# One step of a learning loop in a new order: gradients in one piece, weights 20 from an early sum

## What is computed

```
def _mlp(params, h):                      # params: (w1_0, w2_0), (w1_1, w2_1); hidden width 256
    for w1, w2 in params:
        h = h + gelu(h @ w1) @ w2
    return h
assoc_loss = lambda p, k, v: mean((_mlp(p, k) - v) ** 2)
def step(carry, x_t):                     # 32 steps, one after the other
    params, mom = carry
    k, v = l2norm(x_t @ Wk), x_t @ Wv
    lr, forget, eta = ...                 # one number for each image
    g = grad(assoc_loss)(params, k, v)
    new_mom    = eta * mom - lr * g
    new_params = params * (1 - forget) + new_mom
```

## Time and profile before

| what | before |
|---|---|
| median of 3 runs | 959.83 us (956.37 to 960.83) |
| the profiled execution | 957.53 us, its span 955.7 us |
| busy, share of the span | PE 85%, DVE 76%, ACT 65%, POOL 64% |
| the learning loop | about 72 to 564 us of the span |
| before it, `prepare`; behind it, read-out, attention, experts | 72 us; 392 us |

### The profile page before, as it was taken

The page is one execution under the profiler, slowest core; times in us unless marked ns, Lnnn a source line. Parts: engine busy times, 40 slices in busy tenths (PEclk is TensorE's granted clock), DMA queues, the critical chain, the costliest instruction groups (busy, mean ns, idle before and its releaser), DMA issues. The chain is left out here.

```text
span 955.7 us, 25199 instructions
## 1 busy us (share of the span) xinstructions
PE 809.4 (85%) x8049; PEld 506.4 (53%) x8049; DVE 726.0 (76%) x1861; ACT 618.9 (65%) x1384; POOL 608.6 (64%) x758
## 2 busy tenths in 40 slices
PE   2788999999999999999999989965678777999950
PEld 2455555555555555555555544431246544999940
DVE  3586888888888888888888871578798875777747
ACT  4577777778777787877777753228823523888830
POOL 1127888878788887878788739940004777666650
PEclk8899999999999999999999999987998978999985
DMA  7006999996000000000000005005000113233327
GB/s 239 1 2 140 159 208 158 81 6 2 0 0 0 0 0 0 0 0 0 0 0 0 0 5 157 18 11 185 1 4 29 52 51 90 82 93 93 92 68 239
DMA packets 105406, 54.10 MB, mean 57 GB/s; under 512 B 42624, under 2 KB 96664, under 8 KB 105360
## 3 DMA queue, kind: packets, MB, share of 16 engines
q1 hardware_dynamic: 98976, 43.34, 28.9%
q0 software_dynamic: 4544, 9.38, 3.0%
q10 hardware_dynamic: 1840, 0.79, 0.3%
HBM read 21.49 MB, written 29.44 MB: 53 GB/s over the span
## 5 line engine op out<-in xcount | busy, mean ns | idle before, releaser
L398 POOL TENSOR_TENSOR s_w<-s_xsh,s_w_mem 128x512 f32<-128x512 f32 x186 | 252.0, 1355 | 9.0 <-DVE s_w_mem L570 3.5
L570 DVE SCALAR_TENSOR_TENSOR s_w_mem<-s_w_mem,s_eta,lp_g 128x256 f32<-128x256 f32 x496 | 218.0, 476 | 23.9 <-PE lp_g L733 18.6
L495 ACT ACTIVATE s_xsh<-s_w,l_keep_lr 128x256 f32<-128x256 f32 x384 | 173.9, 507 | 17.5 <-POOL l_keep_lr L418 17.5
L1489 POOL DMA_INDIRECT f_yg<-f_yr,f_xmeta x78 | 78.3, 1004 | 38.4 <-DVE f_yr L1857 25.6
L1484 POOL DMA_INDIRECT f_xg<-f_xrow,f_place x64 | 64.0, 1000 | 49.3 <-DVE f_place L1750 30.4
L403 POOL TENSOR_TENSOR s_xsh<-s_w,l_keep 128x512 f32<-128x512 f32 x64 | 72.0, 1125 | 0.0
L1464 ACT ACTIVATE f_hh<-fp_v,f_bcol 128x256 f32<-128x256 f32 x156 | 61.4, 476 | 14.4 <-DVE f_hs_lo L1848 8.5
L489 ACT COPY l_wt<-lp_b 128x512 f32<-128x512 f32 x96 | 56.5, 588 | 15.0 <-PE lp_b L719 15.0
L719 PE MATMUL lp_b<-s_cst,s_w 128*128 128x128 f32 x384 | 61.7, 284 | 0.0
L1594 PE MATMUL fp_v<-f_xf,s_w_hi 128*128 128x256 bf16 x312 | 54.4, 276 | 3.3 <-DVE f_xmeta L1837 2.7
L707 PE MATMUL lp_h<-s_w,l_gf 128*32 128x128 f32 x1024 | 41.4, 278 | 18.3 <-ACT l_gf L482 18.3
(11 more groups left out here) (360 smaller groups left out, 2040.7 us busy)
## 6 DMA issues: line engine op xcount, KB each, us to landing
f_xg<-s_pad SPq DMA_DIRECT2D x1, 17280.0 KB, 108.2
f_xt<-f_xg SPq DMA_DIRECT2D x39, 130.0 KB
r_w<-in_L_ffn_W_dram SPq DMA_DIRECT2D x16, 256.0 KB, 3.2
s_w<-f_yg SPq DMA_DIRECT2D x16, 256.0 KB, 3.8
xs<-in_x_dram SPq DMA_DIRECT2D x4, 512.0 KB, 7.0
t_w<-in_L_ffn_W_dram SPq DMA_DIRECT2D x8, 256.0 KB
out_dram<-s_x SPq DMA_DIRECT2D x8, 256.0 KB, 3.1
s_xsh<-s_xl SPq DMA_DIRECT2D x4, 448.0 KB, 3.5
```

Of the source, the lines that this page charges most:

```text
L398: nc.gpsimd.tensor_tensor(W[k][:, half(h), :], KW[k][:, half(h), :], M[k][:, half(h), :], ALU.add).then_inc(w_ready[k], 1)
L495: m = nc.scalar.mul(KW[k][:, b, :], W[k][:, b, :], keep_lr[:, b:b + 1])
L570: i = nc.vector.scalar_tensor_tensor(out=M[k][:, b, :], in0=M[k][:, b, :], scalar=eta[:, b:b + 1], in1=ps_g[b][:, 0:256], op0=ALU.mult, op ...
L1489: nc.gpsimd.indirect_dma_start(sb["yg"][:, :], bass.IndirectOffsetOnAxis(ap=xmeta[:, j, a, 0:1].bitcast(mybir.dt.int32), axis=0), yr[j % R ...
```

## The change

All gradients are made for the four batches at once. The four banks become one tensor `ps_all`. The new W20 no longer comes from KW + M: VectorE sums P = eta M + KW for each batch before the gradient is there (`decayed_20`), and then W20 = P + gradient in one instruction over all four banks (`update_20`); the momenta of 20 are still formed, behind or around it. Gradient 10 moves behind the transpose of `h1`. TensorE makes gradient 21 ahead of the transpose of `dp`, and gradient 20 behind up DG0. VectorE does three momenta of 21 instead of one ahead of `da1`. ScalarE's copies and decays and GpSimd's sums, copies and scalings are put in a new order; momenta, decays and sums are counted one by one, in the order of the lists KEEPS, HALVES and MOMENTA. GpSimd's subtraction that made `keep` becomes a copy. The last step follows in its order. The diff, cut to its core:

```diff
-        ps_g = [bank(f"g{b}") for b in range(B)]
+        ps_all = bank("g", B)
+        ps_g = [ps_all[:, 512 * b:512 * b + 512] for b in range(B)]
...
-        G21, G11, G20, G10 = range(4)
-        D21, D11A, D11B, D20A, D20B, D10 = range(1, 7)
+        D21, D11, D20, D10 = range(1, 5)
+        KEEPS = {"21": (0, 2, 3, 1), "20": (0, 1, 2, 3), "10": (2, 0, 1, 3), "11": (0, 1, 2, 3)}
+        HALVES = {"21": (1, 0), "11": (0, 1), "10": (0, 1), "20": (0, 1)}
+        MOMENTA = [("21", 2), ("21", 3), ("21", 0), ("21", 1), ("11", 0), ("11", 3), ("11", 2), ("11", 1),
+                   ("20", 0), ("20", 3), ("20", 1), ("20", 2), ("10", 0), ("10", 1), ("10", 2), ("10", 3)]
...
-                def add(t, k, n, h):
-
-                    pool.wait_ge(kept[k], t * 2 + h + 1)
-                    pool.wait_ge(mom_ready, mom(t, n, h))
-                    nc.gpsimd.tensor_tensor(W[k][:, half(h), :], KW[k][:, half(h), :], M[k][:, half(h), :], ALU.add).then_inc(w_ready[k], 1)
+                def add(t, k, h):
+
+                    pool.wait_ge(kept[k], kept_of(t, k, of_half(h)))
+                    pool.wait_ge(mom_ready, mom(t, k, of_half(h)))
+                    nc.gpsimd.tensor_tensor(W[k][:, half(h), :], KW[k][:, half(h), :], M[k][:, half(h), :], ALU.add).then_inc(w_ready[k], 2)
...
+                def keep_for(t):
+                    nc.gpsimd.tensor_copy(keep[:, :], step_of(t, "coef")[:, 4:8]).then_inc(keep_in, 1)
...
                         for k in ("21", "20", "10"):
-                            pool.wait_ge(kept[k], p * 2 + 2)
-                        pool.wait_ge(kept["11"], p * 2 + 2)
+                            pool.wait_ge(kept[k], kept_of(p, k, range(B)))
+                        pool.wait_ge(ke_ready, t)
+                    else:
+                        keep_for(t)
+                    nc.gpsimd.tensor_copy(kx[:, :], step_of(t + 1, "kf")).then_inc(kx_ready, 1)
                     nc.gpsimd.tensor_copy(keep_lr[:, :], step_of(t, "coef")[:, 4:9]).then_inc(lr_in, 1)
-                    pool.wait_ge(lr_in, t + 1)
-                    nc.gpsimd.tensor_tensor(keep[:, :], keep_lr[:, 0:B], none[:, :], ALU.subtract).then_inc(keep_in, 1)
                     if grads:
-                        add(p, "21", G21, 1)
-                    if grads:
-                        pool.wait_ge(grad_done, p * 6 + D10)
-                    nc.gpsimd.tensor_copy(kc[:, :], step_of(t, "ktok")).then_inc(kc_ready, 1)
-                    if grads:
-                        add(p, "11", G11, 1)
+                        add(p, "11", 0)
                     keep_of(t, "11", 0)
                     if grads:
-                        add(p, "10", G10, 0)
-                    nc.gpsimd.tensor_copy(kx[:, :], step_of(t + 1, "kf")).then_inc(kx_ready, 1)
-                    if grads:
-                        pool.wait_ge(mom_ready, mom(p, G10, 1))
-                    nc.gpsimd.tensor_copy(eta[:, :], step_of(t, "coef")[:, 0:4]).then_inc(eta_in, 1)
+                        add(p, "11", 1)
+                        pool.wait_ge(grad_done, p * 4 + D10)
+                    nc.gpsimd.tensor_copy(kc[:, :], step_of(t, "ktok")).then_inc(kc_ready, 1)
+                    keep_of(t, "11", 1)
                     pool.wait_ge(mm_done, t * 7 + A0)
                     pool.wait_ge(kx_ready, t + 1)
+                    pool.wait_ge(keep_in, t + 1)
+                    scaled(kk, keep).then_inc(kk_ready, 1)
+                    if grads:
+                        add(p, "10", 0)
+                        pool.wait_ge(mom_ready, mom(p, "10"))
+                    nc.gpsimd.tensor_copy(eta[:, :], step_of(t, "coef")[:, 0:4]).then_inc(eta_in, 1)
+                    if grads:
+                        add(p, "10", 1)
+
+                def backward(t):
+                    add(t, "21", 1)
+                    keep_for(t + 1)
                     pool.wait_ge(eta_in, t + 1)
                     scaled(ke, eta).then_inc(ke_ready, 1)
-                    scaled(kk, keep).then_inc(kk_ready, 1)
-                    keep_of(t, "11", 1)
-                    if grads:
-                        add(p, "10", G10, 1)
-
-                def backward(t):
-                    add(t, "21", G21, 0)
-                    pool.wait_ge(mm_done, t * 7 + A0)
+                    add(t, "21", 0)
-                    add(t, "11", G11, 0)
...
                 def forward(p, grads=True):
                     t = p + 1
+                    hidden(t, 0, ps_a)
+                    wt(t, X21A, "21", 0)
+                    feature(t, TG0, gf[0], 256)
+                    keep_of(t, "20", 0)
                     keep_of(t, "21", 0)
-                    hidden(t, 0, ps_a)
                     square(0, ps_a)
-                    feature(t, TG0, gf[0], 256)
-                    wt(t, X21A, "21", 0)
+                    wt(t, X21B, "21", 1)
+                    feature(t, TH1, h1f, 128)
                     tanh(t, 0, ps_a)
                     keep_of(t, "21", 2)
-                    wt(t, X21B, "21", 1)
-                    feature(t, TH1, h1f, 128)
-                    wt(t, X20B, "20", 1)
 
                 def backward(t):
                     hidden(t, 1, ps_b)
                     square(1, ps_b)
+                    wt(t, X20B, "20", 1)
                     feature(t, TG1, gf[1], 256)
                     wt(t, X11A, "11", 0)
                     tanh(t, 1, ps_b)
-                    keep_of(t, "21", 1)
+                    keep_of(t, "20", 1)
+                    keep_of(t, "21", 3)
                     wt(t, X20A, "20", 0)
                     feature(t, TDP, dpf, 128, 0.5)
+                    keep_of(t, "20", 2)
+                    keep_of(t, "20", 3)
+                    keep_of(t, "10", 2)
+                    wt(t, X11B, "11", 1)
+                    feature(t, TDA1, daf, 256)
+                    keep_of(t, "21", 1)
+                    feature(t, TDH1, dh1f, 128, 0.5)
                     keep_of(t, "10", 0)
-                    keep_of(t, "20", 0)
+                    keep_of(t, "10", 1)
+                    keep_of(t, "10", 3)
+
...
+                        if k != "20":
+                            dve.wait_ge(w_ready[k], weights_of(t, k, b // 2))
+                        nc.vector.scalar_tensor_tensor(out=M[k][:, b, :], in0=M[k][:, b, :], scalar=eta[:, b:b + 1],
+                                                       in1=ps_g[b][:, 0:256], op0=ALU.mult, op1=ALU.add).then_inc(mom_ready, 1)
+
+                def decayed_20(t, b):
+
+                    dve.wait_ge(eta_in, t + 1)
+                    dve.wait_ge(kept["20"], kept_of(t, "20", (b,)))
+                    dve.wait_ge(mom_ready, mom(t - 1, "20", (b,)))
+                    nc.vector.scalar_tensor_tensor(out=P[:, b, :], in0=M["20"][:, b, :], scalar=eta[:, b:b + 1],
+                                                   in1=KW["20"][:, b, :], op0=ALU.mult, op1=ALU.add).then_inc(decayed_ready, 1)
+
+                def update_20(t):
+
+                    dve.wait_ge(decayed_ready, 4 * t + 4)
+                    dve.wait_ge(grad_done, t * 4 + D20)
+                    nc.vector.tensor_tensor(W["20"][:, :, :], P[:, :, :],
+                                            ps_all[:, :].rearrange("p (b n) -> p b n", b=B)[:, :, 0:256], ALU.add).then_inc(w_ready["20"], 4)
...
                 def forward(p, grads=True):
                     t = p + 1
-                    if grads:
-                        update(p, "20", G20, 0)
-                        momentum(p, "20", D20B, (2, 3))
-                        update(p, "20", G20, 1)
-                    slope_in(t, 0, ps_a)
-                    weighted(t, 0)
...
+                    if grads:
+                        momentum(p, "20", D20, 2)
+                    slope_in(t, 0, ps_a)
...
+                    weighted(t, 0)
+                    if grads:
+                        momentum(p, "10", D10, 0)
                     bent(t, 0, ps_a)
-                    if grads:
-                        momentum(p, "10", D10, (0,))
                     slope(t, 0, ps_a)
                     if grads:
-                        momentum(p, "10", D10, (1, 2))
+                        momentum(p, "10", D10, 1)
                     slope_in(t, 1, ps_b)
                     if grads:
-                        momentum(p, "10", D10, (3,))
+                        momentum(p, "10", D10, 2, 3)
...
-                    momentum(t, "21", D21, (0,))
+                    momentum(t, "21", D21, 2, 3, 0)
                     slope_times(t, 1, ps_a, DG1)
-                    momentum(t, "21", D21, (1,))
-                    momentum(t, "21", D21, (2, 3))
-                    momentum(t, "11", D11A, (0, 1))
+                    momentum(t, "21", D21, 1)
+                    decayed_20(t, 0)
+                    decayed_20(t, 2)
+                    momentum(t, "11", D11, 0)
                     dve.wait_ge(mm_done, t * 7 + DH1)
```

(69 more changed lines are left out.)

## The result

The changed kernel takes 991.81 us (median of four runs, 988.98 to 994.75) against 958.1 for the kernel before on the same chip (four runs, 955.81 to 960.83): a ratio of 1.0355 with a 95% interval of 1.032 to 1.039. The forecast was 953.0 with a range of 943 to 964. The profiled execution of the changed kernel took 994.75 us, with a span of 992.9, which is 37.2 more than before.

What follows compares the result with a forecast made beforehand. No single engine but a dependency chain of matmul and eviction was taken as the bound; link differences summed to -0.18 a step, 31 x -0.18 = -5.6 on 957.53, 951.9, given as 953.0; range 943 to 964.

Steps and rivals of the forecast that it cites:

- `dp` to `da1`: Backward link: 1.59 to the first momentum, then three momenta ahead of `da1`; 2.89 against 2.14 before, largest loss, 0.75.
- Rival 1: W11 late for up A1 through the port GpSimd and VectorE share: 15.46 a step, +7 us, 964; chance 0.13.
- early sums: VectorE's four 128x256 sums before the gradient: 0.48 alone or 0.44 in a row, hidden in waits for gradient 11 and `dh1`.
- Up A1 at 4.40: Forward link: up A1 starts 4.40 after A0, set by gradient 10 starting at 3.75 and holding TensorE for 0.65.
- The margin of 0.1: GpSimd's W11 whole at 4.3 after A0, up A1 wanting it at 4.40; the margin was 0.2 before.
- One piece of gradients: Four batches cost TensorE what two did, saving 1.3 us a step; shorter links after down DH1 and ahead of A0.
- The wide update: VectorE's 128x1024 sum reading PSUM, taken as 1.23, between 1.23 less 0.1 and 1.9; shared port expected free.
- W20 is in time: The wide sum ends 2.0 after A0 and down H1 wants W20 at 2.19: cover 0.2.
- the walk: The dependency chain of one step followed from A0 to the next A0: 15.06 us a step, 0.18 less than before.
- Prologue and tail, "zero, give or take 1 us": Outside the loop: last step loses a few tenths to a W10 decay wait and wins as much; counted zero.

Runs made afterwards that it cites:

- e1: The changed kernel with one wait added: GpSimd's second sum of W10 waits until VectorE has made layer 1's `dd`; 946.58 us, ratio 0.9888.
- e6: The changed kernel with GpSimd's first sum of W11 ahead of the small copies and the `kx` copy behind its second, no added wait; 938.6 us, ratio 0.9773.
- e3: The changed kernel with two matmuls nobody reads put where TensorE waits for `da1`; 975.86 us, ratio 1.0183.
- e5: The changed kernel with W11's first sum ahead of GpSimd's small copies, and its second W10 sum waiting for layer 1's `dd`; 945.82 us, ratio 0.9833.
- e2: The changed kernel with layer 1's `dd` reading its second input from PSUM instead of SBUF, which alters that gradient; 942.93 us, ratio 0.9858.
- e7: The changed kernel with GpSimd's second W10 sum waiting for `dd`, and two momenta of 21 ahead of `da1` instead of three; 957.36 us, ratio 0.9974.
- e4: The kernel before with three extra VectorE operations, results unread, between `dp` and `dd`; 1136.55 us, ratio 1.188.

## Why the prediction was wrong, point by point

1. *`dp` to `da1`, walked as 2.89, was 3.70.* This is the step that failed. Its wording was: "in the new order GpSimd has only a four-column copy at that place, so I take 1.59". The copy was there (313.35), but the second sum of W10 follows it immediately in GpSimd's program, and it was that which met `dd`. Without it the link is 2.77 (e1, e6), so the momenta were costed well and the neighbour was not. The sum's start was never put on the same time axis as `dd`. The evidence was in the trace of before: the `dd` of 0.573 that the prediction noted ran beside GpSimd's product for `kk`, and ended 0.28 behind it, much as it ends 0.29 behind the sum now:

```profile
310.59 0.40 POOL L409 TENSOR_TENSOR l_kk<-l_kx,l_keep 128x128 f32<-128x128 f32 x1
310.70 0.57 DVE L590 SCALAR_TENSOR_TENSOR l_dd<-l_q,l_g 128x256 f32<-128x256 f32 x1
```

2. *Rival 1 had the mechanism and the wrong place.* It looked for the shared port at W11's two sums, priced a meeting at 0.4, and gave it 0.13. The list of VectorE operations with two SBUF inputs was not gone through: there are two kinds in a step, the two `dd` and the four early sums, against six GpSimd sums of 1.27. W11's second sum does meet one of them, the `dd` of layer 0, but the sum is first and it is `dd` that waits, for 0.08 us only (0.49 against 0.41):

```profile
324.66 1.27 POOL L414 TENSOR_TENSOR s_w<-s_xsh,s_w_mem 128x512 f32<-128x512 f32 x1
...
325.72 0.49 DVE L614 SCALAR_TENSOR_TENSOR l_dd<-l_q,l_g 128x256 f32<-128x256 f32 x1
```

   Where GpSimd is first, the price is up to the whole sum, 0.94 here (1.35 - 0.41).
3. *No term for TensorE's clock.* The trace of before had it at 1.00 in the loop with TensorE 96% busy, and the sum took 1.3 us of work out of each step without asking what the clock does then. In the changed kernel TensorE is busy 339.64 of 400 us at a mean clock of 0.95, in e1 356.20 at 1.00. Two matmul groups in the timeline of a long step of the changed kernel show the cost; at full clock the same two take 0.71 and 0.64:

```profile
333.79 1.22 PE L754 MATMUL lp_g<-l_da,l_h 32*128 32x256 f32 x8
334.94 1.08 PE L735 MATMUL lp_h<-l_wt,l_daf 128*32 128x128 f32 x16
```

   There the granted clock is 0.50 (the window of 334 to 337 us below): the engine at 1.2 GHz instead of 2.4, after a step in which it had been busy 13.3 of 15.8 us. What it did just before is in the same step: from `dp` to `da1` it was busy 2.72 of 3.70 us. Over the same link it was busy all of the 2.14 us before, and 2.25 of 2.77 in e1. Windows of the kernel before, of e1, and two of the changed kernel (columns as above):

```profile
310.43:312.57 2.14, 2.14 (x31) 1.25 (x30) 1.99 (x5) 1.93 (x6) 2.14 (x4) 1.00 0.00 0
```

```profile
303.78:306.55 2.77, 2.25 (x31) 1.34 (x30) 2.62 (x8) 2.40 (x7) 1.55 (x3) 1.00 0.00 0
```

```profile
334.00:337.00 3.00, 3.00 (x33) 1.46 (x33) 2.11 (x6) 0.66 (x2) 2.61 (x5) 0.50 0.00 0
329.23:332.93 3.70, 2.72 (x33) 1.50 (x31) 3.55 (x7) 2.96 (x8) 1.49 (x3) 1.00 0.00 0
```

   All 13 falls of the clock in the changed kernel's loop come 0.6 to 1.2 us after a `da1`, right behind TensorE's idle time of 0.85, and none elsewhere in a step. The Trainium skill, TensorE: Matmul & The Clock Gate, section "What's actually happening", says that the clock goes between these two levels by how busy the engine has lately been; e3, where idle filled with unread work removed every long step, agrees. Fewer gradient groups alone did no harm: with the collision gone and the groups still few, e1 kept the full clock.
4. *Up A1 at 4.40 was 4.54.* W11 was whole at 4.30 after A0, exactly as forecast (308.86 + 1.27 - 305.83). But up A1 didn't start at the recorded end of the sum that released it; 0.24 lay between. The margin of 0.1 was therefore none, and the sign that the prediction gave for its rival 1, up A1 released by W11's sum, was seen though no collision held that sum. With e6's move this link is 2.28 instead of 2.45.
5. *What was right.* One piece of gradients: up DG0 comes 1.77 after down DH1 and A0 1.21 after that, walked as 1.90 and 1.30 (before 2.68 and 1.64), and TensorE's busy time per step fell from 14.58 to 13.25 in e1, 1.33 against the 1.3 forecast. The wide update takes 1.208 to 1.217, taken as 1.23, and the GpSimd sum beside it doesn't hold it up; the early sums take 0.48 (median; one in each step meets the end of a GpSimd sum and takes 0.66, off the chain). W20 is in time: down H1 is released by `gf0` and not by the sum. For a kernel that differs from the changed one by a single wait the walk had the sign and half of the size: 15.06 a step forecast and 14.86 measured in e1, against 15.24 before; 953.0 us against 946.6, which lies inside the stated range. There up A1 came 0.25 later than walked, and the other links together 0.45 earlier (down H1 0.10, `da1` 0.12, up DG0 0.13, A0 0.09). So the agreement is in part errors that cancel.
6. *Prologue and tail, "zero, give or take 1 us".* The first `dp` came 2.2 later, in a stretch from 76 to 84 us whose granted clock was 0.50 instead of 0.79 before. It occurs in some of the profiled executions with nearly the same code there and not in others (first `dp` at 84.1 to 84.2 in the changed kernel, e3 and e5, at 80.2 to 81.0 in e1, e2, e6 and e7). One execution of each was profiled, so whether it belongs to the kernel or to the execution isn't known.

Which steps of the changed kernel get the low clock isn't settled either: 30 of its 31 steps have the same wait and 13 the fall, and the one step of e6 with that wait kept the full clock. What is shown is that idle time of TensorE brings it about: filled, the falls are gone (e3), and enlarged in the old order, they appear (e4). Whether the length of the one wait or TensorE's busy share over a longer time counts, no run separates.

## What to carry to other kernels

Before an operation is moved on VectorE or GpSimd, list VectorE's operations with two SBUF inputs on the critical chain, and lay each against the start times of GpSimd's long ones in the new order; where they meet, let GpSimd wait for the short one (one wait, 45 us here), or give the VectorE operation an input in PSUM. When a change takes work from a TensorE that runs near full, add a term for the clock: here one new wait of 0.85 us a step cost 16 us more, through the clock, than the same wait filled with unread work. A releaser's recorded end isn't the start of what it releases: with 0.24 us between GpSimd's sum and the matmul here, a margin of 0.1 was none.

## What the chip showed that was not expected

- The lock is decided by hundredths of a microsecond, and the loser pays: `dd` first by 0.03 us, `dd` 0.42 and the sum 1.51; the sum first by 0.20, `dd` 1.35 and the sum 1.26. The held `dd` ended 0.28 to 0.29 after the other's recorded end, whether that was a sum of 1.27 or a product of 0.40.
- The width of a VectorE operation did not decide the collision, its inputs did: 128x1024 with one input in PSUM was free beside a whole GpSimd sum (1.21 and 1.27), 128x256 with both in SBUF lost 0.94.
- TensorE's clock fell to half for a part of 13 of 31 steps although its longest idle time in any step of the loop was the 0.85 ahead of the transpose of `da1`, and two unread matmuls in that gap made the kernel 16 us faster (991.8 to 975.9).
- Three short operations ahead of `dd` cost the kernel before 178 us (1136.55 - 958.4), for some 42 us of added work (31 x 1.35), since collision and clock came on top (e4).
